# A weight product in three rounded passes instead of one full-precision pass, in the opening of a fused decoder layer

## The reference, cut to what matters

```
q = input_seq @ Wq.T + bq          # Wq, Wk: 512 x 512
k = condition_seq @ Wk.T + bk
scores = q @ k.T
attn = softmax(scores);  out = attn @ (condition_seq @ Wv.T + bv)
```

## Time and profile before

| what | value |
|---|---|
| time, median of 3 runs | 1396.66 us (1396.48, 1396.66, 1399.25) |
| profiled execution's own time | 1398.64 us |
| its span | 1396.9 us |
| PE busy | 1372.4 us, 98% of the span |
| PEld, DVE, ACT, POOL busy | 1204.7, 869.3, 730.5, 576.0 us |
| MATMUL records of the four blocks of M (line 346) | 32 of 9969 |

### The profile page before, as it was taken

The page is one execution under the profiler, slowest core; times in us unless marked ns, Lnnn a source line. Parts: engine busy times, 40 slices in busy tenths (PEclk is TensorE's granted clock), DMA queues, the critical chain, the costliest instruction groups (busy, mean ns, idle before and its releaser), DMA issues.

```text
span 1396.9 us, 28347 instructions
## 1 busy us (share of the span) xinstructions
PE 1372.4 (98%) x9969; PEld 1204.7 (86%) x9969; DVE 869.3 (62%) x1911; ACT 730.5 (52%) x2005; POOL 576.0 (41%) x475
## 2 busy tenths in 40 slices
PE   7999999999999999999999999999999999999997
PEld 3677777777799999999999998999999999999775
DVE  4589999999765655654564472445443454536697
ACT  4488888888665566556656554222222222322232
POOL 2476767666467665657566620000000000010264
PEclk9999999999999999999999999999999999999999
DMA  7024323336379899989997963011010100000353
GB/s 215 16 66 108 98 63 102 105 82 169 112 195 197 196 230 216 199 203 215 213 209 185 254 184 102 0 27 27 0 26 0 26 16 17 31 1 31 106 189 121
DMA packets 141651, 159.07 MB, mean 114 GB/s; under 512 B 70400, under 2 KB 78592, under 8 KB 141568
## 3 DMA queue, kind: packets, MB, share of 16 engines
q1 hardware_dynamic: 133888, 157.96, 45.0%
q10 hardware_dynamic: 7680, 0.03, 0.4%
HBM read 106.57 MB, written 35.80 MB: 102 GB/s over the span
## 4 chain that ended last, share of the span: by engine, by line
PE 66%; issue 3%; POOL 2%; DVE 1%; ACT 1%; DMA 0%; POOLq 0%; DVEq 0%; ACTq 0%
PE banks L1611 16%; PE banks L1640 11%; PE banks L1046 9%; PE banks L1062 9%; PE banks L1642 6%; PE banks L1031 6%; PE banks L1078 5%; PE banks L1016 1%; POOL o_r L2186 1%; PE banks L2072 1%; PE banks L1094 1%; POOL o_rstd L2194 1%; PE banks L2103 0%; PE banks L2054 0%; DMA x_scratch<-a_xn 0%
## 5 line engine op out<-in xcount | busy, mean ns | idle before, releaser
L461 ACT ACTIVATE s_p<-banks,a_nmax 112x224 f32<-112x224 f32 (+1 forms) x512 | 198.1, 412 | 60.2 <-DVE a_nmax L572 60.1
L759 POOL TENSOR_TENSOR s_p<-s_p,a_rinv 112x896 f32<-112x896 f32 (+1 forms) x128 | 164.6, 1306 | 119.0 <-DVE a_rinv L580 115.9
L1585 POOL CAST m_hi<-w_raw 128x2048 fp32r<-128x2048 f32 x1 | 2.3, 2262 | 407.7 <-PE banks L1611 407.7
L1728 ACT ACTIVATE f_gate<-f_gate 128x448 f32<-128x448 f32 x90 | 52.1, 579 | 198.7 <-DVE f_gate L1851 198.7
L1446 POOL TENSOR_TENSOR s_ct<-s_ct_raw,s_ct 128x750 fp32r<-128x750 f32 x60 | 109.1, 1847 | 102.1 <-ACT s_ct L1167 102.1
L1848 DVE TENSOR_TENSOR f_gate<-banks,f_xg_early 128x448 f32<-128x448 f32 x45 | 28.1, 624 | 189.5 <-PE banks L1642 189.5
L1453 POOL TENSOR_TENSOR x_cx_lo<-s_cx_raw,x_cx_hi 125x512 fp32r<-125x512 f32 x96 | 122.2, 1313 | 25.4 <-ACT x_cx_hi L1195 25.3
L571 DVE TENSOR_REDUCE a_nmax<-banks 112x1 f32<-112x224 f32 x256 | 97.9, 383 | 24.7 <-PE banks L277 23.9
L461 ACT ACTIVATION_READ_ACCUMULATOR s_p<-banks,a_nmax 112x1 f32 x512 | 111.8, 218 | 0.0
L294 PEld LDWEIGHTS banks<-identity,s_p 112*112 112x112 f32 x768 | 87.8, 134 | 21.6 <-issue 2.1
L294 PE MATMUL banks<-identity,s_p 112*112 112x112 f32 x768 | 105.0, 260 | 1.2 <-POOL s_p L759 0.7
(11 more groups left out here) (254 smaller groups left out, 3645.8 us busy)
## 6 DMA issues: line engine op xcount, KB each, us to landing
s_ct_raw<-in_ct SPq DMA_DIRECT2D x16, 1500.0 KB, 7.2
s_cx_raw<-in_cx SPq DMA_DIRECT2D x16, 1344.0 KB
a_xt<-in_xt SPq DMA_DIRECT2D x16, 448.0 KB, 6.4
a_xrow<-in_x SPq DMA_DIRECT2D x16, 448.0 KB, 6.0
a_xres<-in_x SPq DMA_DIRECT2D x16, 448.0 KB, 6.7
x_scratch<-a_xn SPq DMA_DIRECT2D x16, 448.0 KB, 3.3
out<-o_y SPq DMA_DIRECT2D x28, 256.0 KB, 2.0
s_ahead<-x_scratch SPq DMA_DIRECT2D x14, 448.0 KB
```

The lines of the kernel that those rows point to most:

```text
L461: e = act.activation((p1 if c else p0)[:, g, h, :], src, ACT.Exp, bias=nmax[:, g % 2, c, h:h + 1], accum_out=rsum[:, g % 2, c, h:h + 1])
L759: pool.tensor_tensor(p[:, g, :, :], p[:, g, :, :], inv, ALU.mult).then_inc(norm_done, 1)
```

## The change

M is computed from rounded parts in three passes: each block is now twelve fp32r matmuls instead of four float32 ones. Both weight matrices are split whole, in the opening: `wq_hi` by ScalarE at the end of step 1, `wk_hi` by GpSimd after its `normalise` of step 1, `wq_lo` by VectorE in step 2 and `wk_lo` by VectorE in step 3. The two low parts use the buffers `wv_hi` and `wv_lo`, so the splitting of the value weights moves from steps 4 to 7 to steps 7 to 10, after the last block; and since it shares GpSimd with the parts for z, `ZS` becomes 7, so z(5) and z(6) are plain float32. The first block moves within step 3 from slot 1 to slot 4, behind `pv` and `t(n-2, 2)`.

```
-        ZS = 5
+        ZS = 7
+        wq_parts, wk_parts = (shared.wqk_hi[0], shared.wv_hi), (shared.wqk_hi[1], shared.wv_lo)
```

More of the change, by code:

```diff
@@ L243, in z @@
                 if in_parts(m):
-                    wait(pe, parts_done, 2 * m + 2)
+                    wait(pe, parts_done, 2 * (m - ZS) + 2 * KC + 4)
                     pe.matmul(ps_z[:, 0:2 * T], a_hi[:], z_hi[:], start=True, stop=False)
@@ L343, in job @@
                     dk = j - MP
[L344 to L348, removed]
+                    part, k = divmod(piece, KC)
+                    if dk == 0 and k == 0:
+                        pe.wait_ge(spread, KC + (2 if part == 2 else 1))
+                    q, w = wq_parts[part == 1], wk_parts[part == 2]
+                    mm = pe.matmul(ps_w[:, :], q[:, k, 128 * dk:128 * dk + 128], w[:, k, :], start=(piece == 0), stop=(piece == 3 * KC - 1))
+                if piece == (KC if j == KB else 3 * KC) - 1:
                     mm.then_inc(job_mm, 1)
@@ L354, in early @@
                     job(WU + 2 * n + slot // 5, 0)
-                if 2 <= n <= 6 and slot == 1:
+                if n == 2 and slot == 1:
                     for piece in range(KC):
+                        job(KB, piece)
+                if 3 <= n <= 6 and slot == (4 if n == 3 else 1):
+                    for piece in range(3 * KC):
                         job(KB + n - 2, piece)
@@ L543, in steps @@
                         first_columns()
+                    if isinstance(n, int) and n == 1:
+                        act.wait_ge(raw_in[0], 16)
+                        act.activation(wq_parts[0][:], raw[0][:], ACT.Copy).then_inc(prep_act, 1)
                     if g == 0:
@@ L645, in early @@
                     job_out(WU + 2 * n)
+                if middle and n == 2:
+                    dve.wait_ge(prep_act, 2)
+                    dve.tensor_tensor(wq_parts[1][:], raw[0][:], wq_parts[0][:], ALU.subtract).then_inc(spread, 1)
+                if middle and n == 3:
+                    dve.wait_ge(const_ready, 10)
+                    dve.tensor_tensor(wk_parts[1][:], raw[1][:], wk_parts[0][:], ALU.subtract).then_inc(spread, 1)
                 if not middle and n in (1, 2):
@@ L734, in early @@
             def early(n):
-                if 4 <= n < 4 + KC:
-                    k = n - 4
+                if n == 1:
+                    pool.wait_ge(raw_in[1], 16)
+                    pool.tensor_copy(wk_parts[0][:], raw[1][:]).then_inc(const_ready, 1)
+                if 7 <= n < 7 + KC:
+                    k = n - 7
                     if k == 0:
                         pool.wait_ge(raw_in[2], 16)
+                        pool.wait_ge(job_mm, JOBS)
                     pool.tensor_copy(shared.wv_hi[:, k, :], raw[2][:, k, :]).then_inc(parts_done, 1)
@@ L746, in query_parts @@
                 pool.tensor_copy(z_hi[:], xt[:, odd, 2 * j:2 * j + 2, :]).then_inc(parts_done, 1)
-                wait(pool, parts_done, 2 * m + 1)
+                wait(pool, parts_done, 2 * (m - ZS) + 2 * KC + 3)
                 pool.tensor_tensor(z_lo[:], xt[:, odd, 2 * j:2 * j + 2, :], z_hi[:], ALU.subtract).then_inc(parts_done, 1)
@@ L2250 @@
     bk_all: object
+    wqk_hi: object
     x1_odd_in: object
@@ L2381, in decoder @@
                 x1_in=sem("x1_in"), pad_done=sem("pad_done"), ct_in=sem("ct_in"), cx_in=sem("cx_in"), stored=sem("x1_stored"), p0=p0, p1=p1, ct_hi=ct_hi, ct_lo=ct_lo,
-                x1t_first=x1t_first, zt_first=zt_first, wu_raw=wu_raw, bk_all=at("bk_all", 2 * CT, [128, KC, R], F32), x1_odd=at("x1_odd", wu_at - arena_at, [R, TC, D], F32),
+                x1t_first=x1t_first, zt_first=zt_first, wu_raw=wu_raw, bk_all=at("bk_all", 2 * CT, [128, KC, R], F32),
+                wqk_hi=tuple(at(f"wqk_hi{i}", 2 * CT + 4 * KC * R + W * i, [128, KC, D]) for i in range(2)), x1_odd=at("x1_odd", wu_at - arena_at, [R, TC, D], F32),
                 ahead=at("ahead", wu_at - arena_at + 4 * TC * D, [R, TC, D], F32),
```

## The result

The changed kernel takes **1403.68 us** (median of 7 runs, 1400.99 to 1404.40). The kernel before, run beside it, takes 1399.25 (7 runs, 1396.48 to 1401.27). The ratio is 1.0035, 95% interval 1.0024 to 1.0046: slower by 0.35%, and outside the range of 1393.4 to 1398.7. The profiled execution took 1403.68 with a span of 1401.9, 5.0 us longer than that of the kernel before.

The account below looks back on a forecast made before the run. PE was taken as the bound, with the blocks of M on its path. Step 3 +0.7, blocks -2.28 and z(5), z(6) +0.14 gave -1.4 us, from the median 1396.66 to 1395.3 us; range 1393.4 to 1398.7.

Parts of the forecast that it names:

- the sentence on the block: Steps 3 to 6: the block of M is on PE's path; its saving reaches the end unless another wait replaces it.
- Step 3: Opening, first block moved later: its third pass waits 1.4 us for wk_lo, making the step 0.7 us longer.
- The blocks: Steps 4 to 6: twelve rounded matmuls take 2.84 us per block, saving 0.79, 0.70 and 0.79, 2.28 us in all.
- z(5) and z(6): Projections turned float32: 0.93 us instead of 0.86, so 0.07 each, 0.14 us for both.
- The splits, GpSimd in steps 4 to 10: Opening splits hidden or costed at nothing; GpSimd's moved value-weight work also nothing, bounds -0.2 to +0.4 us.
- The clock: Step 5's clock fall costs the profiled execution 3.07 us; the median of 1396.66 was taken to be without it.
- The subtraction as the bound: Rival, step 3: a longer VectorE subtraction for wk_lo stalls PE; 1397.6 us if it takes 4.61; chance 0.07.
- the 131 ns: Rival, the blocks: matmuls issue every 131 ns, saving 4.2 us in all, 1391.1 us; chance 0.02.
- The softmax chain as the bound: Rival, steps with blocks: the softmax chain decides their length, so PE's savings are lost; 1397.5 us; chance 0.05.
- The fall gone: Rival, opening: the median before had the clock's fall and the change loses it; 1392.3 us; chance 0.10.
- the fall in the median: Rival, opening: the clock's fall comes to lie in the changed kernel's median; 1398.3 us; chance 0.24.
- The slower side: Prediction's label for the rival on VectorE's wk_lo subtraction in step 3: 1397.6 us, 0.9 over before; chance 0.07.

Follow-up runs that it names:

- e8: The changed kernel with all four blocks of M as float32 matmuls from the raw matrices, split parts made but not read; 1398.22 us against 1398.09 for the kernel before.
- e12: The changed kernel with only the last two blocks of M in rounded passes, loops kept; 1396.71 us against 1397.61 for the kernel before.
- e5: The kernel before with 12 more instructions (met waits) at the head of TensorE's list; 1397.72 us against 1398.09.
- e9: The changed kernel with the first block in float32 at its old place and z(7), z(8) in float32 too; 1399.44 us, ratio 1.0018 to the kernel before.
- e15: The kernel of e9 run once more, unchanged; no separate time is given.
- e13: The kernel before with 13 more instructions ahead of TensorE's first work; 1403.28 us, ratio 1.0029, runs in two groups.
- e14: The kernel before with 15 more instructions ahead of TensorE's first work; 1403.27 us, ratio 1.0035.
- e6: The changed kernel with the first block of M as four float32 matmuls at its old place in step 3; 1403.55 us, ratio 1.0042 to the kernel before.
- e1: The kernel before with 26 instructions of padding (met waits) at the head of TensorE's list; 1404.59 us against 1397.23.
- e2: The changed kernel with 100 more instructions (met waits) at the head of TensorE's list; 1404.27 us, ratio 1.0051 to the kernel before.
- e10: The kernel before with 26 more instructions (met waits) inside the body of TensorE's cross-attention loop; 1403.84 us, ratio 1.0048.
- e3: The changed kernel with TensorE's cross-attention loop written out; 1397.99 us, ratio 1.0007 to the kernel before.
- e4: The kernel before with TensorE's cross-attention loop written out; 1397.43 us, ratio 1.0005 to the kernel before.
- e7: The kernel of e6 with TensorE's cross-attention loop written out; 1396.63 us against 1398.09 for the kernel before.
- e11: The kernel of e3 with VectorE's subtraction for wk_lo in four signalled quarters; 1397.09 us, ratio 0.9997 to the kernel before.
- e16: The kernel of e3 run again, unchanged; 1397.07 us against 1397.83 for the kernel before.

## Why the prediction was wrong

**The step that failed** is the sentence on the block, "The block is on the path, and what it gives up goes to the end, unless another wait takes its place", as it was used: the sum was made over steps 1 to 10, where the change's instructions are, and everything behind them was taken as the same. The other wait was there, 500 us later: 3.65 us at the jump back, and 5.5 with what the clock added. It depends on the number of TensorE's instructions, which I counted for time and never for length. All thirteen traces of kernels that keep the loop agree. Where the jump stands it takes 7.67 to 8.78 us, nine packets of instructions follow from 565 to 690 us, and there are 58 in all; where it doesn't, it takes 0.21 to 0.22 us, none is moved from the jump to 690 us, and there are 49.

| list | stall at the jump, in the traces | kernels |
|---|---|---|
| -6, 0, +11, +12 | none | e8, before, e12, e5 |
| +13 | none; 4.87 us | e9 and e15; e13 |
| +15 | 3.85 us | e14 |
| +19, +26 | 3.60 to 3.95 us | e6, the changed kernel, e1 |
| +126 | none | e2 |
| 0, body +26 | 3.82 us | e10 |
| no jump | none | e3, e4, e7, e11, e16 |

The Trainium skill (Runtime: NRT & Kernel Launch, Instruction fetch mechanics) says that TensorE's instruction memory holds 2048 instructions, is refilled in blocks of 256 in sequence, and that a taken branch to a page outside the window forces a fetch. By its figures the body of 1634 instructions touches seven or eight of eight blocks, and it is eight for 97 of 256 positions; an estimate from that page. The table agrees: a stall from +13 on, none at +126, and the same from the other end in e10. The packets show that the body is kept in one case and loaded anew in the other. That loading runs ahead and drops the block the jump needs is my reading of why eight is too many; no run shows which block is dropped, or why the boundary is blurred by a few instructions. The page also speaks of a window of two pages; a body of over six that is jumped back over for nothing (in the kernel before) doesn't fit that. Its advice, to write loops out, held: e3 and e7 pay nothing. The other two loops of TensorE, of 1008 and 697 instructions, never stood: in all 18 traces their jumps back take 0.21 to 0.25 us.

**Its price** has two parts. The jump's group is 3.81 longer, 3.65 of it the stall. The granted clock then falls to 0.57 over 588 to 592 us, which makes the next group 1.72 longer. Together 5.5; less what the changed kernel was ahead, 0.38, that is the 5.15 at the group of 617 us.

**The opening, term by term.**
- Step 3: forecast +0.7, measured +0.69. The stall was 1.10, not 1.4, since the first two passes took 2.09 and not 1.90 and the subtraction started 0.1 earlier in the step; a slower third pass (1.03, not 0.95) took it back.
- The blocks: forecast 2.84 us each, from twelve matmuls of the output gate, measured 3.00 (42.48 to 45.48 in step 4, 58.91 to 61.91 in step 6). Steps 4 and 6 give 0.64 each (0.79 forecast); step 5 at the full clock 6.11 against e5's 6.77, 0.66 (0.70). In all 1.94 for 2.28. Of the 0.16 per block 0.12 lies in the third pass (1.03 us up to the next instruction, 0.91 in the output gate), and what follows is of another shape in the two places; no run separates that.
- z(5) and z(6): 0.14 each and not 0.07, half of it in z (0.77 for 0.70) and half in the transposes ahead of it (0.39 for 0.32). I compared records of z alone. With it steps 8 and 10 take 5.28, over the 5.2 that I had set as a sign of being wrong.
- The splits, GpSimd in steps 4 to 10: nothing, by e8 and by steps 7, 9 and 11 (5.00, 4.97, 4.99).
- Sum 0.69 - 1.94 + 0.28 = -1.0 for a forecast of -1.4. It would have been "no change" as well.

**The clock.** I took the median for an execution without a fall. e5 shows that one without is 1395.09, so the median of before (1397.23 to 1399.25 in five sets of runs) has about one in it. The falls lie at 46 to 60 in most traces, at 20 to 28 in the changed kernel, e3 and e9, and at 64 to 70 in e6, e11, e12 and e15. No trace with four float32 blocks has one in the last two places. Window of step 7 of e12:

```profile
63.50:70.04 6.54, 6.54 (x57) 4.60 (x57) 2.83 (x10) 4.51 (x21) 4.07 (x4) 0.74 0.44 139
```

5.00 would be its length at the full clock. Added up by windows of 2 us, the first 90 us have 3.8 us at the lower clock on average in the eight traces with four float32 blocks (0, 0, three of 3.4, three of 6.8), and 6.1 in the ten with rounded ones (two of 3.4, eight of 6.8). That may be where the gain of 1.0 goes. It is a pattern over 18 executions, and no run isolates its cause. The mean granted clock of all runs doesn't settle it: 0.9956 to 0.9960 in e3, e7, e11 and e12, 0.9963 to 0.9967 in the kernels before beside them, but 0.9965 in e16, the kernel of e3, and 0.9958 in e8, whose blocks are float32. It stays open.

**The rivals.** The subtraction as the bound and the 131 ns are out (2.28 us; 250 ns a matmul). The 3.36 us of the earlier trace rows was no spread: GpSimd ran an addition from 815.92 to 818.33 when this subtraction started at 817.1. In the same way the subtraction for `wq_lo` takes 2.48 us in e8 and e16, where it starts 0.3 us before GpSimd's multiply ends, and 2.28 where GpSimd is done. The softmax chain as the bound is out too: step 5 takes 6.11 us at the full clock. "The fall gone" and "the fall in the median" both took the clock as one event that is there or not; it comes in two lengths and several places. The slower side had its sign right and its mechanism wrong. None of the rivals reached behind step 10.

**What beats both.** e7, three blocks rounded, the first as before and the loop written out, has the lowest median (1396.63 against 1398.09 beside it); e12 gives 1396.71 with the loop kept. Neither can be told from the kernel before.

## What to carry to other kernels

An edit has two sizes, its time and its number of instructions. Where a long loop of TensorE's list follows it, however far behind, count both, and look in the new trace at how long each jump back takes, at idle time that ends by "issue" behind it, and at the packets of the instruction queue. If they rise, pad the unchanged kernel by as many instructions before you explain anything by the edit. The result can depend on a handful of instructions in either direction, so a body of this length that runs only twice is better written out (e3, e7) than left to luck.

## What the runs showed of the hardware that was not expected

- The jump back takes 0.2 us or 7.7 to 8.8, of which PE feels nothing or 3.6 to 4.9 us, with 49 or 58 packets of instructions. Near the boundary (list +13) one and the same kernel does one or the other: e13's runs lie at 1397 to 1399 and at 1403 to 1407.
- A wait that is already met isn't free where TensorE has nothing else to do: 200 of them, two to an instruction, put off its first matmul from 5.01 to 11.84 us, so at most 0.12 us for each instruction (11.84 / 100). Twenty-six such instructions (e1) are hidden in the wait for the first weights: 5.17. Fifty-two of them inside the cross-attention's body, among matmuls, cost nothing that can be seen: but for the two at the jump, every group is as long as before, to 0.02 us.
- Each of the six stalls at the jump came with a fall of the clock to half, for 3.4 us in all (stalls of 3.65 in the changed kernel and 4.87 in e13) or for 6.8 (3.60 in e6, 3.82 in e10, 3.85 in e14, 3.95 in e1). In the first two it begins behind the stall, 1.7 and 0.2 us after its end; in the other four it begins while PE stands (e6: 0.50 from 584.1 us, and PE stands until 585.6). The next group then took 30.2 to 31.1 us instead of 28.5, so such a stall costs 1.7 to 2.6 us more than its length.
